# Edge windows begun beside the first feature products of a graph block, on one core

## The reference, cut to what matters

```python
xn = _layernorm(x)
x1 = relu(xn @ W_ah + b_ah)                         # "hidden" features, 1250 x 768
for W, a_s, a_d, b in three layers:                 # 4 heads of 192 each
    h = (x1 @ W).reshape(N, 4, 192)
    as_n, ad_n = (h * a_s).sum(-1), (h * a_d).sum(-1)
    e = leaky_relu(as_n[src] + ad_n[dst])           # per edge, self loops included
    p = exp(e - segment_max(e, dst)[dst])
    alpha = p / segment_sum(p, dst)[dst]
    out = segment_sum(alpha * h[src], dst) + b
```

## Time and profile before

| | us |
|---|---|
| median of 3 runs | 1367.01 (1362.82 to 1367.25) |
| profiled execution, own time | 1366.72 |
| its span | 1364.9 |
| TensorE, VectorE, ScalarE busy | 1294.9, 985.4, 510.1 |
| front ends, first matmul of attention | 193.54 |

### The profile page before, as it was taken

The page is one execution under the profiler, slowest core; times in us unless marked ns, Lnnn a source line. Parts: engine busy times, 40 slices in busy tenths (PEclk is TensorE's granted clock), DMA queues, the critical chain, the costliest instruction groups (busy, mean ns, idle before and its releaser), DMA issues.

```text
span 1364.9 us, 19968 instructions
## 1 busy us (share of the span) xinstructions
PE 1294.9 (95%) x7893; PEld 1223.9 (90%) x7893; DVE 985.4 (72%) x1703; ACT 510.1 (37%) x844; POOL 44.2 (3%) x52
## 2 busy tenths in 40 slices
PE   5899889999997999999999999999999999999886
PEld 5567559999997998999999999999999999999775
DVE  5667849999997525967776767677667776768567
ACT  4434232444435104443324332433343324233373
POOL 5000000000000500000000000000000000000000
PEclk9999989999998999999999999999999999999998
DMA  9210030222215837102010102110211011105003
GB/s 246 85 71 1 0 110 20 92 92 92 73 39 171 231 127 194 38 1 78 1 68 22 63 0 73 39 41 1 73 38 41 0 73 39 43 1 148 1 0 114
DMA packets 23510, 90.13 MB, mean 66 GB/s; under 512 B 3537, under 2 KB 4878, under 8 KB 20347
## 3 DMA queue, kind: packets, MB, share of 16 engines
q1 hardware_dynamic: 22495, 86.57, 19.8%
q10 hardware_dynamic: 924, 2.30, 0.6%
HBM read 77.80 MB, written 11.06 MB: 65 GB/s over the span
## 4 chain that ended last, share of the span: by engine, by line
PE 54%; DVE 7%; ACT 1%; issue 1%; DVEq 0%
PE psum L1753 26%; PE psum L105 8%; PE psum L106 8%; PE psum L107 8%; DVE hN L1377 1%; PE psum L1767 1%; DVE prob L1361 1%; DVE prob L1355 1%; PE psum L1807 1%; DVE acc L1399 0%; DVE x1l L1384 0%; DVE acc L1415 0%; ACT prob L1583 0%; PE psum L1822 0%; DVE xll L1390 0%
## 5 line engine op out<-in xcount | busy, mean ns | idle before, releaser
L1753 PE MATMUL psum<-hN,prob 125*125 125x193 f32 x2400 | 409.0, 327 | 1.5 <-DVE hN L1377 1.5
L1753 PEld LDWEIGHTS psum<-hN,prob 125*125 125x125 f32 x2400 | 395.4, 187 | 2.0 <-issue 1.8
L1583 ACT ACTIVATE prob<-prob,acol 125x1250 f32<-125x1250 f32 x120 | 161.1, 1342 | 381.5 <-DVE prob L1355 381.5
L1361 DVE SCALAR_TENSOR_TENSOR prob<-prob,cnt 125x1250 f32<-125x1250 f32 x120 | 174.7, 1456 | 56.4 <-ACT prob L1583 56.4
L1355 DVE SCALAR_TENSOR_TENSOR prob<-vrow,ncol,urow 125x1250 f32<-125x1250 f32 x120 | 182.0, 1517 | 9.5 <-PE psum L1753 9.5
L796 DVE CUSTOM_DVE_ANT_0 junk<-mask,arow 125x1250 bf16<-125x1250 uint8 x120 | 174.8, 1457 | 3.1
L105 PE MATMUL psum<-woh,xlh 128*125 128x384 f32 x360 | 127.3, 354 | 2.6 <-DVE acc L1399 2.6
L105 PE MATMUL psum<-wph,x1h 128*125 128x384 f32 x330 | 118.5, 359 | 4.8 <-PEq L1012 1.9
L106 PE MATMUL psum<-wol,xlh 128*125 128x384 f32 x360 | 123.0, 342 | 0.0
L107 PE MATMUL psum<-woh,xll 128*125 128x384 f32 x360 | 122.3, 340 | 0.0
L107 PE MATMUL psum<-wph,x1l 128*125 128x384 f32 x330 | 111.9, 339 | 0.0
(11 more groups left out here) (255 smaller groups left out, 2134.4 us busy)
## 6 DMA issues: line engine op xcount, KB each, us to landing
arow<-scratch_a SPq DMA_DIRECT2D x12, 625.0 KB, 4.0
urow<-scratch_uv SPq DMA_DIRECT2D x12, 625.0 KB, 4.1
vrow<-scratch_uv SPq DMA_DIRECT2D x12, 625.0 KB, 6.5
wT<-in_w_turned SPq DMA_DIRECT2D x6, 1152.0 KB, 7.6
wq_raw<-in_w_qkv SPq DMA_DIRECT2D x6, 1152.0 KB, 6.9
wp_raw<-in_w_pair SPq DMA_DIRECT2D x6, 1152.0 KB, 7.6
wo_raw<-in_w_out SPq DMA_DIRECT2D x6, 1152.0 KB, 5.4
xN<-in_x SPq DMA_DIRECT2D x10, 336.0 KB
```

The lines of the kernel that those rows point to most:

```text
L1361: nc.vector.scalar_tensor_tensor(prob[n % RING][:, :], prob[n % RING][:, :], 1.0, cnt[:, n % NT, :], op0=ALU.min, op1=ALU.mult).then_inc(p ...
L1583: nc.scalar.activation(prob[n % RING][:, :], prob[n % RING][:, :], ACT.Exp, bias=acol[:, n // NT, n % NT:n % NT + 1]).then_inc(e_ready, 1)
L1753: last = nc.tensor.matmul(bank(t // 2)[0:P, 193 * (t % 2):193 * (t % 2) + 193], ring[:, t * P:(t + 1) * P], hN[i % 2][:, j, 193 * s:193 * ...
```

## The change

Six things in `front`:

- The three edge loads are issued behind the rows of the second x tile instead of behind all of them.
- VectorE casts the edges at t = 1, makes `tile_f` in halves at t = 2 and 3, the two keys at t = 4, and finds the reach at t = 5 (`find_reach`, the same instructions as before). The transfers of `ends`, its two rows and the reach's row are issued by ScalarE, at t = 2, 3 and 6.
- Windows 0 to 4 (in working order) stand behind hidden products 3 to 7, then two windows to each product from 8 to 17. VectorE makes windows 0 to 3 at t = 6 to 9 of its loop over tiles.
- `wT` keeps two halves instead of four, in the place of x's first tiles; its first load waits until tile 5 is transposed, each later one for the layer before.
- The banks: windows use 6 and 7, hidden products 4 and 5, masks 2, 3 and 1, scores 4, 5 and 0, turned weights 0, turned scores 1.
- Masks are made in the order `MASKS`, from window 13 on and one to a window; the last two stay behind window 24. The turned scores and the minimum of the scores come after window 24's matmuls and one-hot tables, and a mask waits only for the windows that it reads.

```diff
-        wT = [at(f"wT{q}", o, [128, KT, 384]) for q, o in enumerate((0, 9216, S, S + 9216))]
+        wT = [at(f"wT{q}", o, [128, KT, 384]) for q, o in enumerate((S, S + 9216))]
...
-        BESIDE = {8 + j: {2: 3 * j, 4: 3 * j + 1, KT: 3 * j + 2} for j in range(6)}
-        BESIDE.update({14: {KT: 18}, 15: {3: 19, KT: 20}, 16: {KT: 21}, 17: {3: 22, KT: 23}})
-        TAKEN, DENSE = 12, 17
+        BESIDE = {3 + j: {KT: j} for j in range(5)}
+        BESIDE.update({8 + j: {3: 5 + 2 * j, KT: 6 + 2 * j} for j in range(9)})
+        BESIDE[17] = {3: 23, KT: 24}
+        TAKEN, DENSE = 13, 17
         WINDOWS = tuple(range(NW - 1, 2, -1)) + (0, 2, 1)
-        MASKED_AT = {14: (0, 1), 16: (2,), 17: (3,), 18: (4,), 19: (5,), 20: (6,), 21: (7,), 24: (8, 9)}
+        MASKED_AT = {13: (0,), 14: (1,), 15: (2,), 16: (3,), 17: (4,), 18: (5,), 20: (6,), 21: (7,), 24: (8, 9)}
+        MASKS = (7, 6, 9, 8, 5, 4, 3, 2, 1, 0)
...
-        SCORED, HAS = 8, (1, 0, 2, 1, 0)
-        LOW_AT = NW - 1
-        TURNS = ((2, 0, 4), (3, 4, 4), (7, 8, 2))
+        SCORED, HAS = 8, (1, 0, 1, 0, 2)
+        TURNS = ((2, 0, 4), (3, 4, 4), (1, 8, 2))
+        SCORE_BANKS = (4, 5, 0)
...
             x_rows(1)
+            sp.dma_start(chunk_i[:, :], g["dst_c"]).then_inc(edges_in, 16)
+            sp.dma_start(src_i[:, :], g["src_t"]).then_inc(edges_in, 16)
+            sp.dma_start(dst_i[:, :], g["dst_t"]).then_inc(edges_in, 16)
             x_rows(2)
...
             sp.wait_ge(xt_full, 12)
-            sp.wait_ge(wT_in, 32)
-            turned_half(2)
-            turned_half(3)
...
+            for layer in range(LAYERS):
+                if layer:
+                    sp.wait_ge(waT_full, layer)
+                    sp.wait_ge(wT_in, 32 * layer)
+                turned_half(2 * layer)
+                turned_half(2 * layer + 1)
...
+                if t == 5:
+                    find_reach()
+                if t >= 6:
+                    window(t - 6)
             for i in range(2 * NT - 4, 2 * NT):
                 low_part(i)
...
+            for n in range(NT - 6, NW):
+                window(n)
+            dve.wait_ge(at_ready, len(CH))
+            own.done(nc.vector.tensor_reduce(low[:, :], abT[0:HEADS, :], axis=AX.X, op=ALU.min))
+            nc.vector.tensor_scalar(minus_low[:, :], low[:, :], -1.0, None, ALU.mult).then_inc(a_low, 1)
...
+                if t == 2:
+                    act.wait_ge(ends_ready, 1)
+                    act.dma_start(g["dram_ends"].rearrange("e (c u) -> c e u", u=2), ends[:, :, :]).then_inc(ends_in, 16)
+                if t == 3:
+                    act.wait_ge(ends_in, 16)
+                    for k, row in enumerate((lowest_in, highest_in)):
+                        act.dma_start(row[:, :], g["dram_ends"][k].partition_broadcast(NW)).then_inc(ends_in, 16)
+                if t == 6:
+                    act.wait_ge(reach_ready, 1)
+                    act.dma_start(g["reach_row"][0:1, :], reach[:, :]).then_inc(reach_in, 16)
...
+            take_scores()
+            act.wait_ge(wq_in, 16)
+            nc.scalar.activation(g["wq_high"][:, :, :], g["wq_raw"][:, :, :], ACT.Copy).then_inc(wq_ready, 1)
+            take_counts(NW - 1)
             take_columns()
...
-                if i >= 3:
-                    pe.wait_ge(x1_free, i - 2)
+                if i >= 2:
+                    pe.wait_ge(x1_free, i - 1)
...
+                if n == NW - 1:
+                    turn_scores()
+                for q in MASKED_AT.get(n, ()):
+                    turn_mask(q)
...
-            turn_scores()
-            window(NW - 1)
```

More of the change, by code:

```diff
@@ new lines, in _, with window @@
+            units = dve.alloc_register("dve_units")
+            bounds = {}
+            def window(n):
+                w = WINDOWS[n]
+                if n == 0:
+                    dve.wait_ge(reach_in, 16)
+                    dve.sem_inc(hot_free, 2)
+                    dve.reg_mov(units, 0)
+                if n in LOADS:
+                    bounds.update(reaches(n, mybir.EngineType.DVE))
+                pairs, parts = first_pair[n >= TAKEN], first_part[n >= TAKEN]
+                for e in range(CE):
+                    if e % 2 == 0:
+                        if n:
+                            dve.wait_ge(first_free, CE * (n - 1) + e + 2)
+                        nc.vector.tensor_tensor(parts[e // 2][:, :, 0:P], place[:, 0:P].unsqueeze(1).to_broadcast([P, 2, P]),
+                                                part_h[:, bass.ds(bounds[w][0] + e, 2)].unsqueeze(2).to_broadcast([P, 2, P]), ALU.is_equal)
+                    nc.vector.tensor_scalar(pairs[e][:, :], place[:, :], float(WN * w), pair_f[:, bass.ds(bounds[w][0] + e, 1)],
+                                            ALU.add, ALU.is_equal).then_inc(first_ready, 1)
+                if n == DENSE:
+                    dve.sem_inc(hot_free, CE - 2)
+                step = CE if n >= DENSE else 2
+                with dve.Fori(bounds[w][0] + CE, bounds[w][1], step) as unit:
+                    for e in range(step):
+                        slot = (e + step - 2) % CE
+                        if e % 2 == 0:
+                            dve.reg_add(units, units, 2)
+                            dve.wait_ge(hot_free, dve.snap(units))
+                            nc.vector.tensor_tensor(hot_part[slot // 2][:, :, 0:P], place[:, 0:P].unsqueeze(1).to_broadcast([P, 2, P]),
+                                                    part_h[:, bass.ds(unit + e, 2)].unsqueeze(2).to_broadcast([P, 2, P]), ALU.is_equal)
+                        nc.vector.tensor_scalar(hot_pair[slot][:, :], place[:, :], float(WN * w), pair_f[:, bass.ds(unit + e, 1)],
+                                                ALU.add, ALU.is_equal).then_inc(hot_ready, 1)
@@ L391, in _ @@
                     nc.vector.tensor_reduce(ends[:, 1, :], units_of, axis=AX.X, op=ALU.max).then_inc(ends_ready, 1)
-                if t == 7:
-                    own.done(nc.vector.tensor_scalar(tile_f[:, :], src_f[:, :], float(P), None, ALU.is_ge))
-                    for j in range(2, NT):
+                if t in (2, 3):
+                    if t == 2:
+                        own.done(nc.vector.tensor_scalar(tile_f[:, :], src_f[:, :], float(P), None, ALU.is_ge))
+                    for j in range(2, 6) if t == 2 else range(6, NT):
@@ L407, in _ @@
[L407 to L412, removed]
@@ L419, in _ @@
[L419 to L440, removed]
-                step = CE if n >= DENSE else 2
-                with dve.Fori(bounds[w][0] + CE, bounds[w][1], step) as unit:
-                    for e in range(step):
-                        slot = (e + step - 2) % CE
-                        if e % 2 == 0:
-                            dve.reg_add(units, units, 2)
-                            dve.wait_ge(hot_free, dve.snap(units))
-                            nc.vector.tensor_tensor(hot_part[slot // 2][:, :, 0:P], place[:, 0:P].unsqueeze(1).to_broadcast([P, 2, P]),
-                                                    part_h[:, bass.ds(unit + e, 2)].unsqueeze(2).to_broadcast([P, 2, P]), ALU.is_equal)
-                        nc.vector.tensor_scalar(hot_pair[slot][:, :], place[:, :], float(WN * w), pair_f[:, bass.ds(unit + e, 1)],
-                                                ALU.add, ALU.is_equal).then_inc(hot_ready, 1)
@@ L476, in take_x1, with take_score_weights @@
                 act.wait_ge(x1_full, i + 1)
-                nc.scalar.activation(x1T[:, o, c0:c0 + n], bank(4 + i % 3)[:, 0:n], ACT.Relu,
+                nc.scalar.activation(x1T[:, o, c0:c0 + n], bank(4 + i % 2)[:, 0:n], ACT.Relu,
                                      bias=g["bah"][:, o:o + 1]).then_inc(x1_free, 1)
+            def take_score_weights(layer):
+                act.wait_ge(waT_full, layer + 1)
+                for half in range(2):
+                    nc.scalar.activation(waT[:, 384 * half:384 * (half + 1)], bank(2 + half)[32 * half:32 * half + 2 * HL, 0:384], ACT.Copy)\
+                        .then_inc(waT_ready, 1)
```

144 lines of the change are left out of this document (66 added, 78 removed).

## The result

The changed kernel takes 1373.75 us (median of 5 runs, 1372.59 to 1376.63) against 1365.65 us: 1.0061 times as long, 95% interval 1.0044 to 1.0079. It is 8 us slower where no change was forecast, and outside the range.

What follows compares the result with a forecast made beforehand. TensorE was taken to set the front part's pace, with holes from waiting for VectorE. Terms 2.4 + 0.5 − 1.3 − 2.3 + 0.4 = −0.3 on 1366.72 gave 1366.4 us, range 1360.5 to 1372.5.

Steps and rivals of the forecast that it cites:

- The early steps: Front part, VectorE's work per x tile: 2.3 us a step plus inserted casts, keys and reach; reach ready at 30.6.
- The early term: Front part up to score weights and window 4: 67.45 us against 65.05 before, a loss of 2.4 us.
- two allowances: Additions to the early part: +0.5 us for the reach's row in wT's traffic, +0.4 for a clock fall.
- The sum of the chain: VectorE from tile 4's arrival: reach ready at 30.6, its row issued at 33.95, window 0 begun at 38.5.
- The edges: Three edge loads moved ahead of x tile 2: they delay VectorE's statistics of tile 4 by 1.05 us.
- The reach's row: Small transfer sent while wT loads, 4.54 us to the first key before: +0.5 us taken, range 0 to +2.7.
- The ends transfer: Small transfer on ScalarE's queue from 16.7, waited for at 21.5: 4.8 us later, just covered at 4.6.
- rival D: Slower: ScalarE waits for `ends` in the backlog, +10, 1376; decides above 7 us; chance 0.05.
- The clock: TensorE's 4.9 us hole for the reach may drop the clock: +0.4 us taken, bounds 0 to +1.8.
- The middle and the tail: Middle: second mask's wait goes, −1.3 us. Tail, end of scores to attention: 15.4 against 17.7, −2.3 us.
- S + 5.75: Tail: window 24 closes 5.75 us after the end of scores, called S; attention starts at S + 11.7.
- Rival C: Slower: reach's row lands at 4.6 in wT's traffic and the clock falls, 1370.0; chance 0.16.

Runs made afterwards that it cites:

- e2_gpsimd_light: Changed kernel with GpSimd's split of W_ah mostly left out (no low part, one of six slices of the high part copied): 1.0024 of the kernel before.
- e7_keys_beside_gpsimd: Kernel with late keys and edge loads ahead of x tile 2, its casts and keys now made early, GpSimd's work kept: 0.9988 of the kernel before.
- e9_keys_early_light: Kernel with edges first and only casts and keys early, but GpSimd's split of W_ah mostly left out: 0.9951 of the kernel before.
- the light kernels: Kernels that leave out the low part and most of the high part of W_ah, GpSimd's work: 1.0024, 1.0007 and 0.9951 of the kernel before.
- e4_edges_first: Changed kernel with its early half taken back, but the three edge loads ahead of x tile 2: 0.9985 of the kernel before.
- the second profile: The changed kernel run again unedited, for a second profile: 1.0069 of the kernel before.
- e3_wT_later: Changed kernel with one more wait on SP, so the first wT halves load only after the reach's row has landed: 1.0058 of the kernel before.
- e5_light_and_later: Changed kernel with GpSimd's split of W_ah mostly left out and the first wT halves behind the reach's row: 1.0007 of the kernel before.
- e1_late_alone: Changed kernel with its early half taken back (edges, keys, reach, early windows, wT), the late half kept: 1362.52 us, 0.998 of the kernel before.

## Why the prediction was wrong, step by step

- **The early steps failed.** The steps of 2.3 us, the 1.45 for half of `tile_f` and the reach at 30.6 took the durations from rows in which GpSimd was idle (from 31 us on) and put them beside its split of W_ah (11.9 to 30.7). The term left out was +7.2 us in the profile; taking GpSimd's work out is worth 5.0 us of total time in both pairs of kernels (the changed one against e2_gpsimd_light, e7_keys_beside_gpsimd against e9_keys_early_light), and a part of that GpSimd costs with late keys, too. The early term with its two allowances was +3.3 in the sum and is +10.4 in the profile (75.45 against 65.05).
- **The sum of the chain.** The reach was ready 7.5 us late (38.1 for 30.6): 7.2 of stretch and 1.05 more of edges, less 0.8 by which the steps ran shorter than summed. Its row was issued 1.4 us behind it where 3.35 had been taken, because the issue stands at 39.52, at the start of tile 6's normalising, and not behind it and the taking of tile 5; that gave 1.9 back by luck. The row took 2.6 more. Together VectorE's first key is 8.1 late, and from there to the end of window 4 it took 28.8 us, forecast 28.95.
- The Trainium skill (SBUF — State Buffer, Who interferes with whom) has a rule for this: VectorE's second port pair is shared with GpSimd, and whoever issues first holds it for the whole instruction. By it a VectorE instruction with two SBUF inputs contends with a GpSimd instruction that reads SBUF; `cast` and `tensor_scalar` can enter modes that use both port pairs, and then contend too; `tensor_reduce` does not, nor an instruction with at most one SBUF input outside those modes. The trace agrees: `src_f` ended 0.1 us behind a 1.81 us subtraction, `tile_f` and `shift` with two inputs were stretched, the reduction beside the next subtraction kept 0.41 us. In which mode the casts ran no row shows, and the light kernels show that GpSimd's work is the cause, not by which port. The forecast did not weigh the rule.
- **The edges** were mis-sized: tile 2 arrived 2.1 us later (10.30 against 8.19), not 1.05. By e4_edges_first the whole move, with what it gains at t = 6, costs 0.7 (ratios, not clear of none) to 2.1 us (profiles).
- **The reach's row** was mis-sized: +0.5 taken, +2.6 measured, the high end of the range given, and +4.1 in the second profile. Where wT's loads are held back behind the row (e3_wT_later, e5_light_and_later), it took 4.5.
- **The ends transfer.** "Just covered at 4.6" was wrong by size: 8.0 to 9.2 us to the issue that waited for it, in the five profiles that have it there. It cost nothing in the changed kernel only because VectorE was late anyway, and 2.9 us of VectorE's time once it wasn't (e2_gpsimd_light). So rival D's condition (above 7 us) came true and its mechanism was real, at under a third of its price of 10. The Trainium skill's rule weighed there (DMA: Bandwidth & Descriptors, Queues, rings and completion order: separate rings, taken in turns) did not keep it short; no run sent `ends` on SP's queue at that place, so whether the queue or the traffic made it long is not shown.
- **The clock** fell, where +0.4 had been taken for a case left open, and cost about 0.7 us: from the first key to the end of window 0 it took 3.4 us instead of 3.0, and product 4 took 2.5 instead of 2.2. The 28.8 us above hold it, so that their agreement is in part luck.
- **The middle and the tail were right**: −3.9 us by the profile of e1_late_alone, −2.7 by its ratio, for −3.6. No matmul waited for a mask copy between 70 and 150. Window 24 closed 5.8 us after scores (188.64 to 194.4) for S + 5.75, attention began at S + 11.6 for S + 11.7.
- Rival C named the right sign and some of the right pieces (row in traffic, clock), at 1370.0, and its condition, window 0 after 41, came true; the main piece stood in no case.

Open: how the 5 us of the stretch splits over single instructions (it moves with the phase between the two engines), why e3_wT_later gained nothing by ratio although its row was quick, why `ends` takes 8 to 9 us on ScalarE's queue, and what a light kernel with late keys would take. None was tried.

## What to carry to other kernels

Idle time on an engine is not free room: before moving work into a gap, look at what the other engines do in that gap (here GpSimd beside VectorE), and take the duration from a row with them busy. Look in the trace for instructions of one shape with two durations; they say who disturbs whom. Put such work behind the other engine's end and in pieces small enough that the consumer still has work queued: here keys in pieces, with the reach a little earlier, gained about 7 us on the same kernel with keys in one lump (0.993 against 0.998), and with the late half's 2.7 the total is 9.6 us under before. That kernel gives the early windows up; no run shows them paying. A small transfer that other work waits for is better not sent beside bulk loads: the reach's row took 7.1 and 8.7 us beside wT and 4.5 ahead of it.

## What had not been expected of the hardware

- A 0.24 us VectorE cast took up to 1.85 us beside GpSimd; in the changed kernel's profile each of the three casts ended 0.1 to 0.15 us behind the end of a GpSimd instruction. GpSimd's own subtraction stayed at 1.80 to 1.86 us.
- A transfer of 1.2 KB on ScalarE's otherwise empty queue took 8.0 to 9.2 us while SP's x and weight loads ran at about 235 to 255 GB/s, and the way from a row of 0.2 KB to the first key took 8.7 us in the worst profile against 4.5 in quiet.
